# A decoder kernel: one normalisation moved from VectorE to ScalarE, a fused split, and merges at other places

## The reference, cut to what matters

```python
x = x + L0_attn(layernorm(x))                 # attention in a window of 64
x = x + L0_xattn(ctx, ctx, layernorm(x))      # cross attention to 77 context rows
x = x + L0_ffn(layernorm(x))                  # 8 experts, the best 2 of each token
x = x + L1_attn(layernorm(x))                 # causal attention
x = x + L1_xattn(layernorm(x), ctx, ctx)      # cross attention
x = x + L1_ffn(x)                             # quantised gate/up/down products

def _layernorm(x, axis=-1, eps=1e-05):
    m = jnp.mean(x, axis=axis, keepdims=True)
    v = jnp.var(x, axis=axis, keepdims=True)
    return (x - m) / jnp.sqrt(v + eps)
```

## Time and profile before

| | |
|---|---|
| median of 3 runs | 2122.26 us (2119.05 to 2122.82) |
| profiled execution, its own time | 2117.94 us |
| its span, first to last instruction | 2116.1 us |
| granted TensorE clock, mean | 0.972 of full speed |
| busy: TensorE, VectorE, ScalarE, GpSimd | 92%, 59%, 46%, 32% of the span |
| window call, narrow steps | from 8 to 351 us, a step of 18.3 to 18.5 us |
| cross steps behind them | to about 583 us, a step of 13.5 to 16 us |
| experts | to about 1170 us |
| causal call, narrow steps | from 1174 to 1537 us, a step of 20.4 to 20.9 us while expert results are gathered, 19.2 to 19.5 us after |
| its cross steps, the quantised stage | to 1750 us, to the end |

### The profile page before, as it was taken

How to read it: one execution, slowest core, us unless ns; L and a number is a source line. 1 busy time by engine, 2 the same in 40 slices (tenths; PEclk the granted TensorE clock), 3 DMA queues, 4 the chain that set the end, 5 groups by cost and what they waited for, 6 DMA issues and landing times. The chain is left out here.

```text
span 2116.1 us, 57339 instructions
## 1 busy us (share of the span) xinstructions
PE 1949.5 (92%) x19802; PEld 1598.6 (76%) x19802; DVE 1256.2 (59%) x5456; ACT 978.8 (46%) x1905; POOL 685.5 (32%) x1244
## 2 busy tenths in 40 slices
PE   7999998999959999999999798899899998999889
PEld 5888886777748999999999577777777775444377
DVE  5788885777541111111115689988778886369964
ACT  2555555666613333333333355555566653357400
POOL 3666664356560000000001554543422320013400
PEclk9999998999969999999999899999999999999999
DMA  7333332334339999999995634433233330000023
GB/s 223 109 112 109 110 128 82 107 108 132 104 117 407 366 345 341 343 339 340 345 342 201 186 119 131 129 121 124 81 103 111 108 113 29 0 0 0 0 68 92
DMA packets 209555, 334.75 MB, mean 158 GB/s; under 512 B 59501, under 2 KB 193426, under 8 KB 200306
## 3 DMA queue, kind: packets, MB, share of 16 engines
q1 hardware_dynamic: 194914, 301.82, 41.4%
q0 software_dynamic: 9552, 26.10, 4.0%
q10 hardware_dynamic: 4928, 4.72, 0.6%
HBM read 193.74 MB, written 28.05 MB: 105 GB/s over the span
## 5 line engine op out<-in xcount | busy, mean ns | idle before, releaser
L2364 ACT ACTIVATE moe_h<-moe_h_ps,moe_weights 128x128 f32<-128x128 f32 x424 | 132.5, 363 | 255.6 <-PE moe_h_ps L2332 226.1
L2797 PE MATMUL ffn_prod_ps<-x_sb,ffn_weights 128*128 128x512 f32 x480 | 210.9, 599 | 7.0 <-ACT ffn_sig_q L2783 7.0
L2396 DVE TENSOR_TENSOR moe_y<-moe_y_ps,moe_weights 128x256 f32<-128x256 f32 x53 | 22.5, 424 | 328.2 <-PE moe_y_ps L2344 328.2
L1398 ACT ACTIVATE causal_prob<-causal_ps 128x768 f32<-128x768 f32 (+1 forms) x192 | 168.7, 878 | 79.3 <-PE causal_ps L1721 79.0
L2275 POOL DMA_DIRECT2D moe_y_dram<-moe_y x71 | 39.4, 554 | 492.5 <-DVE moe_y L2396 484.3
L2332 PE MATMUL moe_h_ps<-moe_h,moe_weights 128*128 128x128 f32 x1696 | 198.1, 275 | 0.0
L2332 PEld LDWEIGHTS moe_h_ps<-moe_h,moe_weights 128*128 128x128 f32 x1696 | 193.6, 192 | 0.1
L2797 PEld LDWEIGHTS ffn_prod_ps<-x_sb,ffn_weights 128*128 128x128 f32 x480 | 91.1, 192 | 124.6 <-issue 110.4
L1071 DVE CUSTOM_DVE_ANT_0 causal_masked<-causal_ps,causal_causal_mask 128x256 bf16<-128x256 f32 (+1 forms) x512 | 151.9, 351 | 32.0 <-PE causal_ps L1687 31.5
L1071 DVE CUSTOM_DVE_ANT_0 window_masked<-window_ps,window_window_mask 128x160 bf16<-128x160 f32 x512 | 135.1, 319 | 45.8 <-PE window_ps L1687 44.6
L1687 PE MATMUL causal_ps<-k_pair,q_pair 64*128 64x78 f32 (+2 forms) x1024 | 101.6, 299 | 35.6 <-DVE causal_m_tok L1071 26.5
(11 more groups left out here) (424 smaller groups left out, 4776.6 us busy)
## 6 DMA issues: line engine op xcount, KB each, us to landing
moe_weights<-moe_w_in SPq DMA_DIRECT2D x53, 2180.0 KB, 9.7
q_pair<-parts SPq DMA_DIRECT2D x512, 128.0 KB
parts<-moe_w_in SPq DMA_DIRECT2D x17, 2180.0 KB, 9.4
k_pair<-parts SPq DMA_DIRECT2D x256, 128.0 KB
k_pair<-parts SPq DMA_DIRECT2D x256, 38.5 KB
moe_y_dram<-moe_y POOLq DMA_DIRECT2D x71, 128.0 KB, 4.0
moe_rows<-moe_slots_dram SPq DMA_DIRECT2D x53, 128.0 KB, 3.8
x_before_ffn_dram<-x_sb SPq DMA_DIRECT2D x16, 256.0 KB, 2.1
```

What stands on the lines that cost most here:

```text
L1398: nc.scalar.activation(out, src, ACT.Exp).then_inc(expd, 1)
L2364: nc.scalar.activation(out[:, f, :], psum[:, f // 2, (f % 2) * TM:(f % 2) * TM + TM], ACT.Gelu, bias=bias[:, f:f + 1]).then_inc(done, 1)
L2797: op = nc.tensor.matmul(prod_ps[:, slot, f, :].rearrange("p (b t) -> p b t", b=2), w[:, k, at:at + P], x_cols(n // GROUPS, k), start=(k == ...
```

## The change

Three edits, all within `attention`:

1. `next_rows` of narrow steps is taken off VectorE. ScalarE makes the same rows with two activations, `x * rstd + shift`, placed ahead of exponential 6 in the step. GpSimd makes `shift = -(mean * rstd)` with two more small instructions behind `rstd`, and only then lets ScalarE go. In a wide step all stays as it was.
2. `split_max` handles both halves of the partitions in one instruction: one copy and one subtraction where there were two of each. This holds in narrow and wide steps.
3. From step 3 on the merges lie in slots 2, 2, 5 and 7 where they lay in 4, 5, 6 and 7.

```diff
@@ -65,7 +65,8 @@
 
     ln = {n: [sb(f"{n}{i}", [P, ST] + rest, F32) for i in range(2)]
           for n, rest in (("stats", [6]), ("mv", [2]), ("var_eps", []), ("rstd", []))}
-    ln |= {n: sb(n, [P, ST], F32) for n in ("eps", "half")}
+    ln |= {n: sb(n, [P, ST], F32) for n in ("eps", "half", "minus")}
+    ln["shift"] = [sb(f"shift{i}", [P, ST], F32) for i in range(2)]
     return ln
 
 
@@ -419,6 +420,7 @@
         CTX_K = len(k_of_ctx)
         K_FIRST = 2
         K_SLOTS = (3, 5, 6, 7)
+        MERGE_AT = (2, 2, 5, 7)
         START_WARM, END_WARM, LOAD_WARM, DRAIN_WARM = 16, 13, 6, 4
 
         def k_ps(par, L):
@@ -498,6 +500,16 @@
         def turn_ps(ref):
 
             return by_64((psb if route and wide(ref) else psa)[:, :, 0:S])
+
+        def scaled_on_act(ref):
+
+            return ref >= 1 and not wide(ref - 1)
+
+        def chained(t, ref):
+
+            if ref == 0:
+                return 1
+            return 3 * t - 1 if ref <= B + 2 else t + 2 * B + 5
 
         def bias_slot(ref):
 
@@ -688,6 +700,7 @@
             @block.gpsimd
             def _(pool):
                 nc.gpsimd.memset(ln["eps"][:], EPS)
+                nc.gpsimd.memset(ln["minus"][:], -1.0)
                 nc.gpsimd.memset(ln["half"][:], -0.5).then_inc(pool_chain, 1)
                 for L in layers_in:
                     if not L.biased:
@@ -758,8 +771,20 @@
                                             pattern=[[1, P]], channel_multiplier=-1).then_inc(route_filled, 1)
 
                 def layernorm(t, ref):
+                    par = ref % 2
                     pool.wait_ge(stat, t + 1)
-                    inverse_deviation(nc, pool, ln, ref % 2, pool_chain, 1 + t, scaled_by)
+                    n = chained(t, ref)
+                    if not scaled_on_act(ref):
+                        inverse_deviation(nc, pool, ln, par, pool_chain, n, scaled_by)
+                        return
+                    inverse_deviation(nc, pool, ln, par, pool_chain, n, pool_chain)
+                    pool.wait_ge(pool_chain, n + 2)
+                    if ref >= 3:
+                        pool.wait_ge(normed, t - 1)
+                    gate(pool, pool_passed)
+                    nc.gpsimd.tensor_tensor(ln["shift"][par][:], ln["mv"][par][:, :, 0], ln["rstd"][par][:], ALU.mult).then_inc(pool_chain, 1)
+                    pool.wait_ge(pool_chain, n + 3)
+                    nc.gpsimd.tensor_tensor(ln["shift"][par][:], ln["shift"][par][:], ln["minus"][:], ALU.mult).then_inc(scaled_by, 1)
 
                 def add_bias(t, ref):
 
@@ -1036,6 +1061,10 @@
                                                             parts[:, 0, k, 0:nk].bitcast(F32), ALU.add, ALU.subtract)
                     op.then_inc(done, 1)
 
+                def by_pair(cols):
+
+                    return bass.AP(cols.tensor, cols.offset, [list(cols.ap[0]), [64, 2], [1, 4], [maxw, ST]])
+
                 def split_max(t, ref, lag, hf):
 
                     i = t - lag
@@ -1044,14 +1073,10 @@
                     dve.wait_ge(s1_max, before(t, ref, lag) + L.groups // 2 * (hf + 1))
                     if ref - lag >= 1:
                         dve.wait_ge(m_mm, n - 1)
-                    cols = m_cols[:, hf].rearrange("p s c -> p c s")
-                    for ab in range(2):
-                        op = nc.vector.tensor_copy(cols[:, 64 * ab:64 * ab + 4, :], m_tok[:, hf, ab])
-                    op.then_inc(m_hi, 1)
+                    both_halves = lambda first: by_pair(m_cols[:, hf, :, first:first + 4])
+                    nc.vector.tensor_copy(both_halves(0), m_tok[:, hf]).then_inc(m_hi, 1)
                     dve.wait_ge(m_hi, n + 1)
-                    for ab in range(2):
-                        op = nc.vector.tensor_tensor(cols[:, 64 * ab + 4:64 * ab + 8, :], m_tok[:, hf, ab],
-                                                     cols[:, 64 * ab:64 * ab + 4, :].bitcast(F32), ALU.subtract)
+                    op = nc.vector.tensor_tensor(both_halves(4), m_tok[:, hf], both_halves(0).bitcast(F32), ALU.subtract)
                     op.then_inc(m_lo, 1)
 
                 def row_max(t, ref, i):
@@ -1262,7 +1287,7 @@
                     if active(ref, 2) and not (wide(ref - 1) and wide(ref)):
                         split_max(t, ref, 2, 1)
                     for i in range(PAIRS_H):
-                        if i == (4 if wide(ref) else 6):
+                        if i == 4 and wide(ref):
                             next_rows(t, ref)
                         if active(ref, 1):
                             row_max(t, ref, i)
@@ -1332,8 +1357,10 @@
                         if i == 7 and ahead(ref, 6):
                             find_best(t + 1, ref + 1)
                             choose(t + 1, ref + 1)
-                        if i >= 4 and in_merge(ref, 2):
-                            merge_rows(t + 2, ref + 2, i - 4)
+                        if in_merge(ref, 2):
+                            for n in range(4):
+                                if i == (MERGE_AT[n] if ref >= 3 else n + 4):
+                                    merge_rows(t + 2, ref + 2, n)
                         if ref < NL and i == bias_slot(ref):
                             widen(ref)
                     if ref == 0:
@@ -1441,6 +1468,19 @@
                                                   scale=last_ln["rstd"][0][:, s:s + 1])
                     op.then_inc(last_normed, 1)
 
+                def next_rows(t, ref):
+
+                    par = (ref + 1) % 2
+                    rows = in_x(t + 1, ref + 1)
+                    act.wait_ge(scaled_by, t + 2)
+                    if ref >= 1:
+                        act.wait_ge(xT_mm, t)
+                    gate(act, act_passed)
+                    for s in range(ST):
+                        op = nc.scalar.activation(xn[par][:, s, :], rows(t + 1, s), ACT.Identity, bias=ln["shift"][par][:, s:s + 1],
+                                                  scale=ln["rstd"][par][:, s:s + 1])
+                    op.then_inc(normed, 1)
+
                 def keep_turned(t, ref):
 
                     e, par = tail_item(t, 5), (ref - 5) % 2
@@ -1574,6 +1614,8 @@
                         max_rows(t, ref, 1, 0)
                     if tail and in_tail(ref, 5) and wide(ref):
                         keep_turned(t, ref)
+                    if active(ref, -1) and not wide(ref):
+                        next_rows(t, ref)
                     if shift:
                         exponentials(t, ref, 6)
                     if active(ref, 1) and not wide(ref):
```

## The result

The changed kernel takes **2136.27 us** (median of 13 runs, 2129.36 to 2148.91) against 2120.36 us of the kernel before in the same sittings (13 runs); the ratio is 1.0081 with a 95% interval of 1.0065 to 1.0098. Forecast were 2122.7 us, no change that can be told, and a range up to 2129.5. So the kernel is slower by 16 us, and the time lies outside the range. The profiled execution after is one of 2134.74 us (span 2133.0), 16.8 over the profiled execution before.

A forecast was written before the change was run, and what follows sets the result against it. VectorE was taken as a possible limit in causal steps, hardly in window steps. Terms 2.5 + 1.3 + 2.2 - 4.0 - 0.3 + 0.3 - 1.6 = +0.4 us on the median 2122.26 gave 2122.7; range 2114.5 to 2129.5.

The forecast's parts named there:

- causal gather steps: Causal steps 3 to 12: VectorE's gain is taken by GpSimd and ScalarE; -0.4 us a step, -4.0 in all.
- Two things remain: Causal steps 3 to 12: second cut shorter by 0.2 us, next step's slot 1 by 0.4, of which 0.2 counts.
- four cases: No change that can be told 0.46; VectorE's relief, faster 0.28; gathers blocked, slower 0.12; ScalarE later than priced, slower 0.14.
- rival (a): Causal steps 3 to 12: merges block gathers, each step loses up to 0.9 us; about 2129 us; chance 0.12.
- The 0.4 in the next step's slot 1: Causal steps with gathers: scores 1 no longer wait for a merge and the split; 0.4 us goes, 0.2 reaches value products.
- My upper bound: Merges beside gathers in causal steps: at most a merge's length, 0.43 us, twice a step, 8.6 over 10 steps.
- Window steps: Window steps 2 to 15: ScalarE's activations make exponential 6 0.18 us late each step; +2.5 us.
- Window step 17: Once, at window step 17: exponential 6 starts at 346.65 instead of 345.29, delaying what follows; +1.3 us.
- Head of the causal call: Causal step 0, once: context copies start 3.25 us later behind the activations; +2.2 us after slack.
- Cross steps: Cross steps behind the window layer: fused split shortens VectorE's chain by 0.16 us in 10 steps; -1.6 us.
- Rival (c): Causal gather steps: TensorE's waits of 1.0 and 0.7 us go, half kept is -8; 2115 us; chance 0.28.

## Why the prediction was wrong, point by point

**The step that failed** is the one on the causal gather steps: "So what VectorE gives is taken by the chain of GpSimd and ScalarE. Two things remain", -0.4 a step, -4.0. I worked out when shifted scores 7 would start and took TensorE's idle time in front of it as free, since its sum stayed the same. That it would lie in one piece was in my own rows (waits for maxima "moved" to the exponential) and I drew nothing from it. Measured are +11.0 and +13.0 us in steps 3 to 12 (206.4 to 217.4 and 219.4). Of this 9.7 to 11.7 is the clock, since with it kept up the same steps take 207.7. None of my four cases had this mechanism, the clock had no term in the sum at all, and rival (a), whose 2129 is the nearest, had it for another reason.

**The rest of that term, with the clock up**, is +1.3 instead of -4.0 (207.7 against 206.4), so it was mis-sized by 0.5 a step. The 206.4 hold one fall, in step 3, and the 207.7 none; steps 4 to 12, without a fall in either, are 188.2 against 185.8, so 0.3 longer each and mis-sized by 0.7. Placed values to shifted scores 7 were priced at 12.54 us (9.96 from the earlier trace rows, 0.6, 0.13, 0.98 and 0.87), less 0.2 for the cut; step 7 of the changed kernel shows 1341.54 - 1328.68 = 12.86. The two activations hold ScalarE for 1.00, as priced. The shift has reached ScalarE 0.91 after `rstd` ends, not 0.73. The variance's addition on GpSimd takes 0.38 instead of 0.18 and the first gather 1.28 instead of 1.03; both overlap a merge at its new place. (The addition does so only with the fused split: with the merges moved and the old split it takes 0.19.) The second cut gave back 0.2, as I had said. The 0.4 in the next step's slot 1 did come (scores 1 start 1.4 to 1.6 instead of 1.9 us into a step where the clock is up), and went into the wait in front of shifted scores 7.

**Rival (a), gathers blocked by merges**, is half right in mechanism and small in price: with the merges alone the first gather takes 1.14 to 1.29 instead of 1.03, some 0.2 a step and not 0.9, and the kernel is not slower by it. My upper bound was the whole length of two merges, 0.87; the rows show at most some 0.25.

**Window steps** went as forecast in mechanism and size: 18.53 and 18.33 became 18.70 and 18.50, 0.17 to 0.18 each, and shifted scores 7 wait 0.41 instead of 0.25:

```profile
180.02 0.70 ACT L1425 ACTIVATE window_prob<-window_ps 128x640 f32<-128x640 f32 x1
180.60 1.09 ACT L1480 ACTIVATE window_xn<-x_sb,window_shift,window_rstd 128x256 f32 x2
181.59 0.70 ACT L1425 ACTIVATE window_prob<-window_ps 128x640 f32<-128x640 f32 x1
...
182.34 0.42 PE L1758 MATMUL window_ps<-window_m_rows,selects 64*128 64x320 f32 x2 [0.41 <-ACT window_prob L1425]
```

Exponential 6 is 1.57 behind exponential 5 instead of 1.40. Over steps 4 to 15 this makes 1.2 to 1.4 us and not 2.1, because steps 14 and 15, uneven anyway, took 0.2 to 0.4 less together.

**Window step 17** (+1.3): steps 16 and 17 together are 40.6 and 43.5 after against 41.8 and 42.4 before. The delay itself came: exponential 6 starts 350.42 - 347.48 = 2.94 behind exponential 5, where the kernel before has 345.29 - 343.83 = 1.46. But no time can be seen for it in this spread.

**Head of the causal call** (+2.2): the copies start at 1187.19, that is 3.34 later when the call's own later start of 0.5 is taken off; 3.25 was forecast. But the products that wait for them, in ScalarE's and TensorE's order of time after:

```profile
1186.19 1.09 ACT L1480 ACTIVATE causal_xn<-x_sb,causal_shift,causal_rstd 128x256 f32<-128x256 f32 x2 [2.23 <-POOL causal_shift L787]
1187.19 1.55 ACT L1435 ACTIVATE causal_cross_mask_ctxT<-causal_ps 128x512 f32<-128x512 f32 x3
...
1187.82 1.79 PE L1673 MATMUL causal_ps<-ident,usal_cross_mask_ctx_rows 128*128 128x128 f32 x8 [3.19 <-ACT causal_cross_mask_ctxT L1435]
1190.21 5.33 PE L1691 MATMUL causal_ps<-causal_cross_mask_ctxT,causal_cross_mask_wk 128*128 128x462 f32 x8 [0.61 <-ACT causal_cross_mask_ctxT L1435]
```

and before:

```profile
1185.87 3.11 PE L1649 MATMUL causal_ps<-causal_cross_mask_ctxT,causal_cross_mask_wk 128*128 128x462 f32 x8 [0.81 <-ACT causal_cross_mask_ctxT L1408]
```

TensorE idles 3.19 in one piece, and eight products take 5.33 instead of 3.11. Step 0 is 19.7 instead of 14.5, steps 0 to 2 are 4.6 and 5.6 us longer. The lateness was right, and the clock behind it was left out a second time.

**Cross steps** (-1.6): 15.12 became 14.99 with the split alone, 0.13 a step against 0.16 forecast. In the whole stretch the two changed profiles are 0.6 to 4.2 us under the two before, around the forecast. But 2.5 to 3.1 of it is the first wide step, 13.4 instead of 15.9 and 16.4, for which I had no term; with the normalisation alone it takes 13.5, with the merges alone 16.4 and with the split alone 14.6. So that the size of the stretch fits is in part luck.

**Rival (c)**, VectorE's relief comes through, was true of VectorE and false of the step: it needs the gathers out of GpSimd's chain and the fused split, and then it gives more than I had priced (2113 and 2107).

The sum as measured, roughly: 10.7 for the clock in the gather steps (all runs), 1.3 for their rest, about 5 for the head, 1.3 for the window steps, less about 2 in the cross steps: 16.3, where 15.9 were measured. It mixes medians with single profiles, whose stretches differ by up to 4 us, so that it closes so well is partly luck.

## What to carry to other kernels

When a change takes away waits of TensorE but the time of the step is set elsewhere, ask where the idle time goes: the same idle time at another place, in one piece above all, can cost more than it did, since the granted clock can fall behind it. Read the clock by microseconds behind the waits of a step before believing that their sum is all that counts; the longest wait is only a rough sign (behind 0.83 us it fell in one kernel, behind 1.3 us in another it didn't), and work put inside the wait is the test. Relieving one engine pays only if the next limit is known: here GpSimd's chain stood at the same height as VectorE, and one line that moves two gathers behind `rstd` turned the changed kernel's loss of 16 us into a gain of some 7, and of 15 with the normalisation left on VectorE where ScalarE had no room for it.

## What the runs showed of the hardware that I had not expected

- A single wait of TensorE of 1.7 us in a step of 21 was followed by some 3.4 us at 1.2 GHz, in steps where it is otherwise busy nearly all the time. In steps 4 to 12 waits of up to 1.3 us in the kernel before and with the merges alone were followed by none; steps 4 and 5 of the changed kernel, with nearly the same wait, had no fall in one profile and one each in the other. With the split alone a wait of 1.32 was followed by a fall and one of 1.41 was not, and with `next_rows` behind exponential 6 waits of 0.83 in window steps were, in seven of ten. Which waits bring a fall was not settled beyond that.
- Once begun, the falls of the changed kernel come in every further step with gathers, 18.4 and 19.4 us into a step in turn, and the steps alternate between 23.0 and 21.5 us.
- Small instructions of VectorE that read and write SBUF can be held until an instruction of GpSimd ends: two of 8 numbers a row took 1.86 us beside back-to-back cuts in one kernel and 0.62 in another. In the first of them one instruction in place of two was worth 17 us, far more than its busy time says; in the kernel before it cost 3.
- The same holds for a larger one: a `tensor_scalar` of 128x256 took 0.41 us free of a cut and 0.70 to 0.87 beside one.
